# The two sums of a softplus move from VectorE to TensorE

## What is computed

```
x_dbl = xh @ W_x
dt_low, Bmat, Cmat = x_dbl[..., :8], x_dbl[..., 8:24], x_dbl[..., 24:]
dt = jax.nn.softplus(dt_low @ W_dt + b_dt)        # 256 channels
h = exp(dt * A) * h + dt * B * xc                 # 16 states per channel, a scan over the sequence
y = sum over the states of h * C  (+ xc * D)
```

## Time and profile before

| | |
|---|---|
| median of 3 runs | 14764.8 us (14764.23 to 14765.93) |
| the profiled execution | 14764.73 us, span 14762.9 us |
| GpSimd busy | 13802.9 us, 93% |
| VectorE busy | 13568.2 us, 92% |
| TensorE busy | 10835.3 us, 73% |
| ScalarE busy | 10216.6 us, 69% |
| mean granted TensorE clock | 0.858 of full speed |

### The profile page before, as it was taken

The page is one execution under the profiler, slowest core; times in us unless marked ns, Lnnn a source line. Parts: engine busy times, 40 slices in busy tenths (PEclk is TensorE's granted clock), DMA queues, the critical chain, the costliest instruction groups (busy, mean ns, idle before and its releaser), DMA issues.

```text
span 14762.9 us, 147515 instructions
## 1 busy us (share of the span) xinstructions
PE 10835.3 (73%) x32388; PEld 3297.2 (22%) x32388; DVE 13568.2 (92%) x11492; ACT 10216.6 (69%) x16668; POOL 13802.9 (93%) x3076
## 2 busy tenths in 40 slices
PE   2777777777777777777777777777777777777776
PEld 0222222222222222222222222222222222222221
DVE  1999999999999999999999999999999999999999
ACT  5766766767676667667676676767676766766676
POOL 0999999999999999999999999999999999999999
PEclk9888888888888888888888888888888888888887
DMA  5555555555555555555555555555555555555554
GB/s 211 133 135 132 135 132 137 129 137 130 137 132 129 137 130 137 130 136 132 135 132 135 135 130 137 129 137 130 133 134 133 134 133 136 129 138 129 138 130 115
DMA packets 1035849, 1990.52 MB, mean 135 GB/s; under 512 B 120065, under 2 KB 121146, under 8 KB 1030714
## 3 DMA queue, kind: packets, MB, share of 16 engines
q1 hardware_dynamic: 1034810, 1979.41, 56.2%
HBM read 1626.62 MB, written 352.32 MB: 134 GB/s over the span
## 4 chain that ended last, share of the span: by engine, by line
POOL 68%; issue 28%; DMA 1%; ACT 1%; PE 0%; DVE 0%; POOLq 0%; SPq 0%; ACTq 0%; DVEq 0%
POOL hq L914 45%; POOL dbx L906 23%; DMA o<-in_x 1%; ACT o L502 0%; DVE hq L811 0%; POOLq L913 0%; SPq L199 0%; ACT L502 0%; POOLq L905 0%; PE pp L319 0%; PE pp L331 0%; SPq L193 0%; DVE dbx L798 0%; ACT ps_a L575 0%; DMA dtx_d<-sp 0%
## 5 line engine op out<-in xcount | busy, mean ns | idle before, releaser
L914 POOL TENSOR_TENSOR hq<-hq,c_rep 128x2048 f32<-128x2048 f32 x2048 | 9259.9, 4533 | 598.1 <-ACT carry L581 588.6
L811 DVE TENSOR_TENSOR_SCAN hq<-ps_a,carry,dbx 128x512 f32<-128x512 f32 x7168 | 8629.8, 1263 | 180.7 <-issue 101.4
L575 ACT ACTIVATE ps_a<-dt_rep,A_neg 128x512 f32<-128x512 f32 x8192 | 5589.2, 687 | 3852.1 <-DVE hq L811 3813.3
L906 POOL TENSOR_TENSOR dbx<-dtx_rep,b_rep 128x2048 f32<-128x2048 f32 x1024 | 4631.2, 4523 | 340.4 <-DMA dtx_rep<-dtx_d 340.4
L423 PE MATMUL ps_acc<-hq,dsum 128*32 128x512 f32 x16384 | 2337.2, 644 | 22.2 <-POOL hq L914 22.2
L798 DVE TENSOR_TENSOR dbx<-dtx_rep,ps_b 128x2048 f32<-128x2048 f32 x1024 | 2315.4, 2261 | 15.9 <-DMA dtx_rep<-dtx_d 15.9
L331 PE MATMUL pp<-xin,diag 128*128 128x504 f32 (+3 forms) x4608 | 2212.9, 608 | 13.9 <-ACT diag L606 13.9
L354 PE MATMUL pp<-gbuf,w_center 128*128 128x512 f32 x512 | 529.2, 1137 | 1487.7 <-DVE gbuf L764 1487.7
L367 PE MATMUL pp<-x,W_taps 128*128 128x512 f32 x768 | 643.4, 934 | 1197.0 <-DVE x L772 644.7
L411 PE MATMUL ps_b<-dbl,bsel 41*128 41x512 f32 x2048 | 1159.8, 646 | 228.8 <-DVE dbx L798 222.4
L811 DVE TENSOR_TENSOR_SCAN hq<-ps_a,dbx 128x512 f32<-128x512 f32 x1024 | 1179.7, 1204 | 15.3 <-ACT ps_a L575 15.3
(11 more groups left out here) (116 smaller groups left out, 10014.3 us busy)
## 6 DMA issues: line engine op xcount, KB each, us to landing
dt_rep<-dt_d SPq DMA_DIRECT2D x2048, 256.0 KB, 5.3
dtx_rep<-dtx_d SPq DMA_DIRECT2D x2048, 256.0 KB, 5.5
c_rep<-bc_d SPq DMA_DIRECT2D x1024, 256.0 KB, 5.4
b_rep<-bc_d SPq DMA_DIRECT2D x1024, 128.0 KB, 2.9
dt_d<-dt SPq DMA_DIRECT2D x256, 512.0 KB, 6.0
dtx_d<-sp SPq DMA_DIRECT2D x256, 512.0 KB, 2.8
out<-o SPq DMA_DIRECT2D x128, 512.0 KB, 2.7
xin<-in_x SPq DMA_DIRECT2D x192, 320.0 KB, 7.8
```

The lines of the kernel that those rows point to most:

```text
L575: A(ps_a[:, i % RA, :], dt_rep[:, q // NQ, g, :], ACT.Exp, scale=A_neg[:, q // NQ, q % NQ, g:g + 1]).then_inc(exp_done, 1)
L811: v.tensor_tensor_scan(hq[:, q % HQ, g, :], ps_a[:, i % RA, :], dbx[:, slot(q), g, :], carry[:, q, g:g + 1] if c % CH else 0.0, ALU.mult, ...
L906: g.tensor_tensor(dbx[:, slot(q), :, :], dtx_rep[:, d, :, :], b_rep[:, c % 2, q % NQ // 2, :].unsqueeze(1).to_broadcast([P, DG, T]), ALU.m ...
L914: g.tensor_tensor(quad, quad, c_rep[:, c % 2, q % NQ, :].unsqueeze(1).to_broadcast([P, DG, T]), ALU.mult).then_inc(cmul_done, 1)
```

## The change

Half of p is projected: the weights and bias `wdt` are multiplied by 0.5 once, at the start. With h = p / 2 in `pp`, ScalarE writes |h| into `sp`, and TensorE adds it onto `pp` with the unit matrix as weights (h + |h| = max(p, 0)). ScalarE goes on with exp(-2|h|) and ln(1 + ...), now in the tile `dt`, and TensorE adds that onto `pp` too. The new `step_sum` has two matmuls of 128 x 512 (one for each bank), and runs twice for each chunk: in TensorE's slot 13 behind the first, and in slot 16 behind the third instruction of ScalarE. The second gives `step_done`, for which `dt_x` waits. VectorE's `softplus` is gone; `dt_x` moves from slot 16 to 17, ScalarE's `evac_dt` from 17 to 18 and `evac_conv` from 18 to 19. The wait for `dt_out` (the last chunk's DMA out of `dt`) moves from `evac_dt` to the exp.

```diff
-ACT_XZ, ACT_DBL, ACT_SP, ACT_DT, ACT_OUT = 5, 9, (12, 13, 14), 17, 23
-ACT_CONV, ACT_GELU, ACT_SQ, ACT_RSTD = 18, 21, 27, 30
-DVE_NORM, DVE_Y1, DVE_DT, DVE_Y0, DVE_GATE = 0, 8, 16, 24, 25
+ACT_XZ, ACT_DBL, ACT_SP, ACT_DT, ACT_OUT = 5, 9, (12, 13, 14), 18, 23
+ACT_CONV, ACT_GELU, ACT_SQ, ACT_RSTD = 19, 21, 27, 30
+PE_STEP = (13, 16)
+DVE_NORM, DVE_Y1, DVE_DT, DVE_Y0, DVE_GATE = 0, 8, 17, 24, 25
...
+            def step_sum(b, c, k):
+                pe.wait_ge(sp_done, 3 * (b * CH + c) + (1, 3)[k])
+                for d in range(DI):
+                    last = mm(pp[:, d, :], w["ident"][:], (sp, dt)[k][:, d, :], start=False, stop=True, skip_group_check=True)
+                if k:
+                    last.then_inc(step_done, 1)
...
                         if u == PE_DT:
                             step_dt(b, c + 1)
+                        for k in range(2):
+                            if u == PE_STEP[k]:
+                                step_sum(b, c + 1, k)
...
             step_dt(0, 0)
+            step_sum(0, 0, 0)
+            step_sum(0, 0, 1)
...
                     if k == 1:
-                        A(sp[:], sp[:], ACT.Exp, scale=-1.0).then_inc(sp_done, 1)
+                        if not (isinstance(b, int) and b * CH + c == 0):
+                            act.wait_ge(dt_out, 16 * (b * CH + c))
+                        A(dt[:], sp[:], ACT.Exp, scale=-2.0).then_inc(sp_done, 1)
                     else:
-                        A(sp[:], sp[:], ACT.Ln, bias=1.0).then_inc(sp_done, 1)
+                        A(dt[:], dt[:], ACT.Ln, bias=1.0).then_inc(sp_done, 1)
...
-                if not (isinstance(b, int) and b * CH + c == 0):
-                    act.wait_ge(dt_out, 16 * (b * CH + c))
                 A(dt[:], pp[:, 0:2, :], ACT.Copy).then_inc(dt_done, 1)
...
+            v.tensor_scalar(w["wdt"][:], w["wdt"][:], 0.5, None, ALU.mult)
...
-            def softplus(b, c):
-                dve.wait_ge(sp_done, 3 * (b * CH + c + 1))
-                v.scalar_tensor_tensor(pp[:, 0:2, :], pp[:, 0:2, :], 0.0, sp[:], ALU.max, ALU.add).then_inc(step_done, 1)
...
                         if u == DVE_DT:
-                            softplus(b, c + 1)
                             dt_x(b, c + 1)
```

More of the change, by code:

```diff
@@ L874, in _ @@
             add_input(0, 0)
-            softplus(0, 0)
             dt_x(0, 0)
```

## The result

The changed kernel takes 15582.7 us (15581.05 to 15585.09, 4 runs) against 14765.4 us before (4 runs): a ratio of 1.0554, 95% interval 1.0535 to 1.0572. It is 817 us slower, where 901 were forecast. Its profiled execution has a span of 15583.2 us.

What follows compares the result with a forecast made beforehand. VectorE's own work was taken to set a chunk's pace, with TensorE's list full before slot 16. 223 x 3.47 = 774 plus 32 x 3.94 = 126, about 1 at the start, on 14764.7 gave 15665 us; 8-in-10 range 15520 to 15780.

Steps and rivals of the forecast that it cites:

- The bound and the way to the step: VectorE paces a chunk; TensorE's full list from x1 to slot 16 delays dt_x by 4.65 us, 3.47 lost per middle chunk.
- The size of a sum: Each step_sum on TensorE taken like step_dt: 1.91 us where work follows, 1.98 to the end of the last.
- The other chunks: Chunks without carried state lose 3.94 us, 32 counted; the 223 others lose 3.47 us each.
- the last step's loss: The loss at the program's last step, counted among the 255 chunks' losses inside the loops.
- What was costed at nothing: ScalarE's other tile, its dt_out wait, halving wdt once, later evac_dt and the later DMAs: nothing.
- The cover in front of `gelu`: ScalarE's gelu behind step_y: cover shrinks from 1.26 to 0.1 us and holds barely; nothing taken.
- this end of the prediction's range: If gelu's cover fails, the excess goes onto the path through gelu and gate; 0.5 us a chunk kept as other end.
- the second sum is there in time: Rival: TensorE reaches the second sum when the logarithm ends, dt_x starts at 7057.90, time near 14610; 4%.
- its own 130 us: The in-time rival's least gain, some 130 us, after GpSimd's 0.46 us limit in middle chunks.
- `gelu`'s cover: Rival: cover before gelu fails by half a microsecond, 128 us more, 15790; 9% together with the low-clock rival.
- part of the delay is taken up in VectorE's waits for ScalarE: Rival: VectorE's waits before L788 and L768, 431.6 us together, vanish, giving about 15230; 6%.
- the low clock under the sums: Rival: both TensorE sums at low clock, 974 us more, 16640; 9% together with the gelu-cover rival.

Runs made afterwards that it cites:

- one sum of two: Changed kernel with the first sum on TensorE left out, second sum still in slot 16: 15133.8 us in a single run.
- the early sum: Changed kernel with the second sum in TensorE's slot 13, behind that slot's tap, in place of slot 16: 15199.2 us, ratio 1.0294.
- the slots alone: Kernel before with softplus and dt_x in slot 17, evac_dt in 18, evac_conv in 19, no sum on TensorE: 14765.9 us, ratio 1.0001.
- the early sum with the other order: Changed kernel with second sum in slot 13, plus ScalarE's evac_out in slot 21 and gelu in 22: 14555.0 us, ratio 0.9857.

## Why the prediction was right

**The bound and the way to the step.** Right. `dt_x` was forecast to start 30.73 us behind the start of x1 (7062.17 - 7031.44) and starts 30.46 behind it (7162.19 - 7131.73); the projections of p come at the same distance as before, 18.12 us (7149.85 - 7131.73 and 7049.56 - 7031.44). That TensorE's list sets this, and not its total load, is shown by one sum of two, and by the early sum, which took the wait from 4.35 to 0.33 us.

**The size of a sum.** This term was mis-sized. The prediction took a `step_sum` like `step_dt`, 1.91 us in the list and 1.98 + 0.12 to `dt_x`, and put its lower bound at the tap's 1.88 us. The trace shows 1.72 us for the first, below that bound, and 2.03 us from the start of the second to `dt_x`: 0.27 us a chunk less, 255 x 0.27 = 69 us. That 41 or 128 rows make no difference was right. What differs is what stands beside the products: `step_dt` has products with weights of another shape in front of it and behind it, the first sum stands between taps whose weights are 128 x 128 like its own (the last section has the numbers), and the tap's 0.94 us was a third of the length of a row, not the step from one product to the next. The nearer row was `step_y`, whose two products start 0.86 us apart:

```profile
7063.54 1.02 PE L349 MATMUL pp<-sq,w_b1T 128*128 128x512 f32 x2
```

The Trainium skill's "FP8 and Floating Point Precision", TensorE Precision Notes, has four passes for a float32 product, and the estimate of 0.85 us that the prediction worked out from it was nearer too, against the 0.86 us measured inside a sum. That it gave a time 100 us below the forecast, and the measured time is 82 below it, is partly luck, since only 69 us come from the size of the sums. Of the mechanism nothing more than the length is shown here.

**The other chunks.** Chunk 1 of the loop loses 2.75 us and not 3.20. Its projections start late, as TensorE must wait for a copy on ScalarE, and in a time of low clock. Before (first fence), the third product of them still took 1.91 us, at a granted clock of 0.50, that is 1.2 GHz; in a chunk 1 of after (second fence) the clock rose during the second, and the third took 1.02 us at a granted clock of 1.00, 2.4 GHz:

```profile
7158.35 1.91 PE L368 MATMUL pp<-x,W_taps 128*128 128x512 f32 x2
7160.05 1.91 PE L367 MATMUL pp<-x,W_taps 128*128 128x512 f32 x2
```

```profile
7553.28 1.51 PE L376 MATMUL pp<-x,W_taps 128*128 128x512 f32 x2
7554.63 1.02 PE L375 MATMUL pp<-x,W_taps 128*128 128x512 f32 x2
```

That chunk takes 57.63 us, like a middle one, and so do 16 of the 31 of its kind; the others take up to 58.7. Why the clock rises sooner there was not tried. In chunk 6 the convolution is at the upper edge of the next image, and three taps with 448 columns stand in front of the sums, so `dt_x` comes 30.14 us behind x1 and the loss is 2.88 us; before, that was hidden behind VectorE. Together these are another 24 us off the forecast (31 x 0.45 and 31 x 0.32). Chunks 5 and 8 lose 0.17 and 0.15 us more than the smaller sum gives, some 10 us back. At the ends of the program the second x1 comes 6.4 us later (351.40 in place of 345.00) where 1 was forecast, but behind the last x1 nothing is lost where the last step's loss was forecast: 2 us back. The spans of the two profiled executions differ by 820.3 us, 81 less than the forecast of 901, and 69 + 24 - 10 - 2 = 81.

**What was costed at nothing.** The later slots cost nothing by themselves (the slots alone), and the slots, the tile of the exp and the later DMAs together cost nothing that shows in the early sum with the other order. The cover in front of `gelu` was forecast to shrink to 0.1 us and to hold, barely. It did in nearly all: in the chunk shown `gelu` starts 0.09 us behind the end of `step_y`, and in the chunks 8 it waits 0.15 us. But in five of the chunks 5 it failed. There TensorE, after a wait of 1.78 us for the copy of the step, did `step_out` at a granted clock of 0.53, in 3.59 us in place of 1.96; `gelu` waited 1.66 us for the end of `step_y`, and `y_gate` 2.56 us in place of 0.90:

```profile
2577.46 3.59 PE L407 MATMUL pp<-y,w_Wout 128*128 128x512 f32 x4 [1.78 <-ACT dt L615]
2582.86 0.69 ACT L533 ACTIVATE gbuf<-pp,w_vec 128x512 f32<-128x512 f32 x1 [1.66 <-PE pp L358]
2587.45 0.69 DVE L798 TENSOR_TENSOR y<-ps_acc,sz 128x512 f32<-128x512 f32 x1 [2.56 <-ACT y L581]
```

These five chunks take 59.18 us and the other chunks 5 57.52, which is why their mean is above that of a middle chunk; the five cost 8 us in all. So this end of the prediction's range was real, and that it cost so little hung on the clock in a few chunks. That the cover was the next thing to give way everywhere was shown by the early sum.

**The rivals.** The rival "the second sum is there in time" was put to the test by the early sum, and its price was wrong as it stood: the prediction had it near 14610 (its own 130 us give 14635), and 15199 came, for `gelu`'s cover fails first. With the order changed as well it is 14555. The rival that part of the delay is taken up in VectorE's waits for ScalarE is out: neither wait is shorter (249.3 us after 235.6, and 196.3 after 196.0). Of the dearer rivals the low clock under the sums is out for the chunk shown: from 7149.80 to 7163.00 the granted clock is 1.00 (the 0.97 over the longer window holds the end of the low clock in the projections), and the means of the two groups over the whole trace, 620 and 596 ns, are near the 618 and 593 of that chunk, so few of the others can have been slow. The other, `gelu`'s cover, came true in the five chunks above.

**Against the change itself.** Taking 1.24 us a chunk off VectorE brought 213 us where nothing was put in its place, since GpSimd is next. The same is to be had by moving `evac_out` in front of `gelu`, at no cost on TensorE.

What stays open: what sets the 12.3 us that GpSimd waits in each image around the group normalisation, and so why the floor gives 30 us more when both the instruction and the wait are gone.

## What to carry to other kernels

An engine that is a quarter idle on average can be full in the stretch that counts: read its list from the event that starts the chain to the place of the new instruction, and add up all in between, for the new work waits behind it and delays all that follows. When a wait is removed, ask at once which cover fails next (here 1.26 us in front of `gelu`), and change both together. And before moving work off the busiest engine, look at what it waits for: 0.9 us a chunk of VectorE's waiting, removed by an order on ScalarE, gave as much as the 1.24 us instruction.

## What the runs showed of the hardware

At a granted clock of 1.00, how far a float32 product of 512 columns moved TensorE's list on went by what stood beside it, and not by its 41 or 128 rows. In the TensorE rows of the result, the first sum stands between taps with weights of its own shape, 128 x 128, and takes 1.72 us of the list for its two products. The second stands behind `select_b`, with weights of 41 x 128, and takes 1.83 us (7161.99 - 7160.16). `step_dt`, 41 x 128 with other shapes on both sides, takes 1.92 us (7151.77 - 7149.85).

The start times of the single records (two to a product) in the trace of the changed kernel say the same. Inside `step_dt` and inside `step_sum` alike, they follow each other by 0.429 us. Where 41 x 128 or 128 x 32 meets 128 x 128, the last record in front of the change takes 0.52 us, and the first of 512 columns with 41 x 128 or 128 x 128 behind it 0.53 (medians of 255 to 1086 records for each kind of change). Other weights of the same shape cost nothing extra, as the two products of `step_y` show, 0.86 us apart. What makes a change of shape dear was not tried.
